# Vision block kernel: the last 64 inner rows of the experts' up layer in plain fp32 on the two row halves

## The reference, cut to what matters

```python
def _L0_ffn_ref(x, router_w, w1, w2):       # x: 2048 tokens x 192
    probs = softmax(xt @ router_w.T)
    topk_w, topk_idx = top_k(probs, 8); topk_w = topk_w / sum(topk_w)
    comb = zeros((T, 16)); comb[t, topk_idx[t]] = topk_w[t]
    for e in range(16):                     # widths: 8 experts of 128, 8 of 256
        h = gelu(xt @ w1[:, off:off + wd])  # up layer, 192 inner rows
        out = out + comb[:, e:e + 1] * (h @ w2[off:off + wd, :])
```

## Time and profile before

| | |
|---|---|
| median of the runs | 721.57 us (721.25 to 721.74) |
| the profiled execution | 722.35 us, of which the span of instructions is 720.5 us |
| TensorE busy | 673.1 us, 93% of the span |
| VectorE busy | 494.9 us, 69% |
| ScalarE busy | 353.7 us, 49% |
| GpSimd busy | 107.3 us, 15% |
| attention part | up to about 477 us |
| expert stage | from there to the end |

### The profile page before, as it was taken

How to read it: one execution, slowest core, us unless ns; L and a number is a source line. 1 busy time by engine, 2 the same in 40 slices (tenths; PEclk the granted TensorE clock), 3 DMA queues, 4 the chain that set the end, 5 groups by cost and what they waited for, 6 DMA issues and landing times.

```text
span 720.5 us, 29763 instructions
## 1 busy us (share of the span) xinstructions
PE 673.1 (93%) x13218; PEld 593.7 (82%) x13218; DVE 494.9 (69%) x1350; ACT 353.7 (49%) x916; POOL 107.3 (15%) x328
## 2 busy tenths in 40 slices
PE   5668999999999999999999999899999999999997
PEld 2557888888888888888888888778999999999996
DVE  5247777777887887778787887667547546646743
ACT  0124565555665665655665656655343443443442
POOL 0121222222222123122123131010000000000000
PEclk9969999999999999999999999999999999999999
DMA  8952111111111111110100000000000000000000
GB/s 310 308 192 61 63 33 32 62 33 34 62 33 34 62 33 35 60 33 32 62 4 4 5 4 5 4 2 1 1 0 23 1 1 23 1 0 23 1 1 22
DMA packets 12255, 30.63 MB, mean 43 GB/s; under 512 B 1120, under 2 KB 7392, under 8 KB 11616
## 3 DMA queue, kind: packets, MB, share of 16 engines
q1 hardware_dynamic: 12128, 28.73, 12.1%
HBM read 27.16 MB, written 1.57 MB: 40 GB/s over the span
## 4 chain that ended last, share of the span: by engine, by line
PE 77%; DVE 15%; ACT 4%; issue 2%; DMA 1%; POOL 0%; DVEq 0%; SPq 0%; POOLq 0%; ACTq 0%
PE ps L371 24%; PE ps L503 17%; PE ps L493 15%; PE ps L270 6%; DVE uu L761 4%; DVE sq L680 3%; PE ps L284 2%; PE ps L321 2%; PE ps L389 2%; PE ps L456 2%; ACT qq L574 2%; DVE rf L768 2%; PE ps L285 1%; ACT rr L578 1%; PE ps L382 1%
## 5 line engine op out<-in xcount | busy, mean ns | idle before, releaser
L820 DVE SCALAR_TENSOR_TENSOR acc<-ps,comb,acc 128x192 f32<-128x192 f32 x256 | 89.1, 410 | 83.9 <-PE ps L503 83.8
L503 PE MATMUL ps<-w_sb,work 128*128 128x192 f32 x768 | 140.4, 326 | 0.7 <-ACT work L651 0.7
L503 PEld LDWEIGHTS ps<-w_sb,work 128*128 128x128 f32 x768 | 129.5, 190 | 9.5 <-issue 1.1
L371 PE MATMUL ps<-rr 64*64 64x64 f32 x3840 | 130.1, 220 | 4.8 <-issue 2.1
L371 PEld LDWEIGHTS ps<-rr 64*64 64x64 f32 x3840 | 118.6, 135 | 17.5 <-ACT rr L578 10.8
L651 ACT ACTIVATE work<-ps 128x512 f32<-128x512 f32 x96 | 57.3, 597 | 137.8 <-PE ps L493 137.8
L574 ACT ACTIVATE qq<-ps 128x384 f32<-128x384 f32 x192 | 92.2, 489 | 63.4 <-PE ps L371 61.2
L761 DVE SCALAR_TENSOR_TENSOR uu<-rr,qq 128x384 f32<-128x384 f32 x160 | 87.8, 558 | 46.2 <-ACT qq L574 40.2
L578 ACT ACTIVATE rr<-ps 128x384 f32<-128x384 f32 x160 | 73.9, 489 | 80.3 <-PE ps L371 79.3
L371 PE MATMUL ps<-uu,qq 64*64 64x64 f32 x4608 | 96.5, 224 | 15.6 <-DVE uu L761 13.7
L371 PEld LDWEIGHTS ps<-uu,qq 64*64 64x64 f32 x4608 | 80.5, 134 | 33.4 <-DVE uu L761 30.2
(11 more groups left out here) (137 smaller groups left out, 1032.5 us busy)
## 6 DMA issues: line engine op xcount, KB each, us to landing
xtb<-xt_dram SPq DMA_DIRECT2D x16, 512.0 KB, 3.6
work<-x_dram SPq DMA_DIRECT2D x16, 512.0 KB, 3.7
wsh<-ws_dram SPq DMA_DIRECT2D x2, 1440.0 KB, 7.7
w_sb<-w_dram SPq DMA_DIRECT2D x1, 2304.0 KB, 25.8
w_a<-w_dram SPq DMA_DIRECT2D x1, 1536.0 KB, 12.5
w_b<-w_dram SPq DMA_DIRECT2D x2, 768.0 KB, 16.7
out_dram<-acc SPq DMA_DIRECT2D x4, 384.0 KB, 2.6
mult<-copies_dram SPq DMA_DIRECT2D x1, 512.0 KB, 13.0
```

The costliest lines, as they stand in the source:

```text
L371: last = pe.matmul(ps[z:z + 64, 2 * lane + i, 64 * j:64 * j + 64], lhs[r, lane, i, j, :], rhs[r, lane, i, j, :], start=True, stop=True)
L503: last = pe.matmul(ps[:, 2 + 2 * (e % 2) + j // 2, (j % 2) * DIM:(j % 2 + 1) * DIM], hid[:, n % 4, j * P:(j + 1) * P], w2_sb[:, c, :], sta ...
L820: last = dve.scalar_tensor_tensor(out=a, in0=ps[:, 2 + 2 * (e % 2) + j // 2, (j % 2) * DIM:(j % 2 + 1) * DIM], scalar=comb[:, g * GT + j, ...
```

## The change

The last 64 inner rows are no longer split into high and low parts. A chunk's full part, `up_full`, keeps the three matmuls on rows 0 to 127. The 64 last rows are one plain fp32 matmul per chunk, `up_half`, straight from w1_b and a new fp32 tile xend; even chunks read the upper half of the partitions (0 to 63), odd chunks the lower half (64 to 127). Two chunks are done together: full, full, half, half. wb is gone, ScalarE and VectorE prepare only wah and wal, ScalarE writes xend beside xhi, and the loops of all three engines step by two chunks, with weights prepared four and five chunks ahead.

```diff
@@ -116,12 +116,12 @@
         acc = sb("acc", [P, NT, DIM])
         comb = sb("comb", [P, NT, EXPERTS])
 
-        xhi, xlo = sb("xhi", [P, 2, NT * P], F32R), sb("xlo", [P, 2, NT * P], F32R)
+        xhi, xlo, xend = sb("xhi", [P, NT * P], F32R), sb("xlo", [P, NT * P], F32R), sb("xend", [P, NT * P])
         hid = work[:].rearrange("p (c n) -> p c n", c=4)
 
         with nc.sbuf_tensor("wsh", [P, 2, 5, 3, DIM], F32) as wsh, nc.sbuf_tensor("whalo", [P, 2, DIM], F32) as whalo:
             pass
-        wah, wal, wb = (sb(n, [P, SLOTS, P], F32R) for n in ("wah", "wal", "wb"))
+        wah, wal = (sb(n, [P, SLOTS, P], F32R) for n in ("wah", "wal"))
 
         ps = ctx.enter_context(nc.psum_tensor("ps", [P, 8, 512], F32))
         A, B, C, D = (ps[:, i, :] for i in (4, 5, 6, 7))
@@ -148,7 +148,7 @@
         q_ready, u_ready, prod_done, r_ready, o_done = sems("q_ready u_ready prod_done r_ready o_done")
         o_copied, proj_done, h2_ready = sems("o_copied proj_done h2_ready")
         tbn_a, tbn_b, trstd, x2_ready, x2tr_done = sems("tbn_a tbn_b trstd x2_ready x2tr_done")
-        x2t_ready, xhi_ready, x2_saved, logits_done = sems("x2t_ready xhi_ready x2_saved logits_done")
+        x2t_ready, xend_ready, xhi_ready, x2_saved, logits_done = sems("x2t_ready xend_ready xhi_ready x2_saved logits_done")
         lmax, lexp, ltop, lrep, lsel, lsum, linv = sems("lmax lexp ltop lrep lsel lsum linv")
         comb_ready, whi_ready, wlo_ready, up_done = sems("comb_ready whi_ready wlo_ready up_done")
         gelu_done, down_done, expert_added = sems("gelu_done down_done expert_added")
@@ -236,7 +236,7 @@
 
             def low_tokens(t):
                 pool.wait_ge(xhi_ready, t + 1)
-                pool.tensor_tensor(xlo[:, :, t * P:(t + 1) * P], x2t[:], xhi[:, :, t * P:(t + 1) * P].bitcast(F32),
+                pool.tensor_tensor(xlo[:, t * P:(t + 1) * P], x2t[:, 0], xhi[:, t * P:(t + 1) * P].bitcast(F32),
                                    ALU.subtract).then_inc(x2_saved, 1)
 
             def iteration(t):
@@ -475,12 +475,12 @@
 
 
             pe.wait_ge(ffw_loaded, 64)
-            def up(n):
+            def up_full(n):
                 g = n // HID
                 if n % HID == 0:
                     pe.wait_ge(x2_saved, (g + 1) * GT)
-                pe.wait_ge(whi_ready, 2 * n + 2)
-                pe.wait_ge(wlo_ready, 2 * n + 2)
+                pe.wait_ge(whi_ready, n + 1)
+                pe.wait_ge(wlo_ready, n + 1)
                 if n >= 3:
                     pe.wait_ge(gelu_done, n - 2)
                 if n == 0:
@@ -488,10 +488,19 @@
                 if n == 1:
                     pe.wait_ge(r_ready, 12 * NT)
                 tok4, k = slice(g * GT * P, (g + 1) * GT * P), n % SLOTS
-                parts = ((wah, xhi, 0), (wah, xlo, 0), (wal, xhi, 0), (wb, xhi, 1), (wb, xlo, 1))
-                for m, (w, xs, half) in enumerate(parts):
-                    last = pe.matmul(ps[:, UPB[n % 3], :], w[:, k, :], xs[:, half, tok4], start=(m == 0), stop=(m == 4))
-                last.then_inc(up_done, 1)
+                for m, (w, xs) in enumerate(((wah, xhi), (wah, xlo), (wal, xhi))):
+                    pe.matmul(ps[:, UPB[n % 3], :], w[:, k, :], xs[:, tok4], start=(m == 0), stop=False)
+
+            def up_half(n):
+                g, r = n // HID, slice(64 * (n % 2), 64 * (n % 2) + 64)
+                tok4 = slice(g * GT * P, (g + 1) * GT * P)
+                pe.matmul(ps[:, UPB[n % 3], :], w1_b[r, n % HID * P:(n % HID + 1) * P], xend[r, tok4], start=False, stop=True).then_inc(up_done, 1)
+
+            def up_pair(n):
+                up_full(n)
+                up_full(n + 1)
+                up_half(n)
+                up_half(n + 1)
 
             def down(n):
                 g, c = divmod(n, HID)
@@ -507,18 +516,19 @@
                 if c == FIRST[e] + WIDTH[e] - 1:
                     last.then_inc(down_done, 1)
 
-            up(0)
+            up_pair(0)
             out_heads(NT - 1)
-            for n in range(NC):
-                if n + 1 < NC:
-                    up(n + 1)
+            for n in range(0, NC, 2):
+                if n + 2 < NC:
+                    up_pair(n + 2)
                 if n == 0:
                     project(NT - 1)
                 if n == 2:
                     transpose_x2(NT - 1)
-                if n == 3:
+                if n == 4:
                     logits(NT - 1)
                 down(n)
+                down(n + 1)
 
 
         @block.scalar
@@ -589,7 +599,8 @@
                     act.wait_ge(x2_saved, t)
                 c = (D if t == NT - 1 else C)[:, 0:2 * P].rearrange("p (a n) -> p a n", a=2)
                 act.activation(x2t[:], c, ACT.Copy).then_inc(x2t_ready, 1)
-                act.activation(xhi[:, :, t * P:(t + 1) * P], c, ACT.Copy).then_inc(xhi_ready, 1)
+                act.activation(xend[:, t * P:(t + 1) * P], c[:, 1], ACT.Copy).then_inc(xend_ready, 1)
+                act.activation(xhi[:, t * P:(t + 1) * P], c[:, 0], ACT.Copy).then_inc(xhi_ready, 1)
 
             def router_exp(t):
                 act.wait_ge(lmax, t + 1)
@@ -597,8 +608,7 @@
 
             def high_part(n):
                 c = n % HID
-                for w, raw in ((wah, w1_a), (wb, w1_b)):
-                    act.activation(w[:, n % SLOTS, :], raw[:, c * P:(c + 1) * P], ACT.Copy).then_inc(whi_ready, 1)
+                act.activation(wah[:, n % SLOTS, :], w1_a[:, c * P:(c + 1) * P], ACT.Copy).then_inc(whi_ready, 1)
 
             def first_window(k, t):
                 if k == 1 and on(t - 1):
@@ -615,10 +625,11 @@
                     exponents(t + 1)
                 if k == 2 and on(t + 1):
                     copy_kernel(t + 1)
-                if k in (0, 1, 2) and t == NT - 1:
-                    if k == 0:
+                if k in (1, 2) and t == NT - 1:
+                    if k == 1:
                         act.wait_ge(ffw_loaded, 64)
-                    high_part(k)
+                    high_part(2 * k - 2)
+                    high_part(2 * k - 1)
                 if k == 3 and on(t - 1):
                     copy_x2(t - 1)
                 if k == 4 and on(t + 2):
@@ -650,16 +661,18 @@
                     act.wait_ge(down_done, g * EXPERTS + EXPERT_OF[c] + 1)
                 act.activation(hid[:, n % 4, :], ps[:, UPB[n % 3], :], ACT.Gelu_apprx_tanh).then_inc(gelu_done, 1)
 
-            for n in range(NC):
+            for n in range(0, NC, 2):
                 gelu(n)
+                gelu(n + 1)
                 if n == 0:
                     copy_out(NT - 1)
-                if n == 3:
+                if n == 4:
                     copy_x2(NT - 1)
-                if n == 5:
+                if n == 6:
                     router_exp(NT - 1)
-                if n + 3 < NC:
-                    high_part(n + 3)
+                for m in (n + 4, n + 5):
+                    if m < NC:
+                        high_part(m)
 
 
         @block.vector
@@ -806,11 +819,10 @@
                 dve.tensor_scalar(comb[:, t, :], rt[:, 3, :], rst[:, 3:4], None, ALU.mult).then_inc(comb_ready, 1)
 
             def low_part(n):
-                dve.wait_ge(whi_ready, 2 * n + 2)
+                dve.wait_ge(whi_ready, n + 1)
                 k, col = n % SLOTS, n % HID * P
-                for w, high, raw, r in ((wal, wah, w1_a, slice(0, P)), (wb, wb, w1_b, slice(DB, P))):
-                    dve.tensor_tensor(w[r, k, :], raw[r, col:col + P], high[r, k, :].bitcast(F32),
-                                      ALU.subtract).then_inc(wlo_ready, 1)
+                dve.tensor_tensor(wal[:, k, :], w1_a[:, col:col + P], wah[:, k, :].bitcast(F32),
+                                  ALU.subtract).then_inc(wlo_ready, 1)
 
             def add_expert(g, e):
                 dve.wait_ge(down_done, g * EXPERTS + e + 1)
@@ -849,9 +861,9 @@
                     router_weights(t - 2)
                 if k == 4 and on(t + 1):
                     start_newton(t + 1)
-                if k in (1, 2, 3) and t == NT - 1:
-                    low_part(k - 1)
-
+                if k in (2, 3) and t == NT - 1:
+                    low_part(2 * k - 4)
+                    low_part(2 * k - 3)
                 if k == 4 and on(t - 1):
                     router_max(t - 1)
                 if k == 5 and on(t + 2):
@@ -907,22 +919,24 @@
             dve.tensor_copy(scrap[:, 2:3], scrap[:, 1:2]).then_inc(expert_added, 1)
             router_weights(NT - 2)
             dve.wait_ge(comb_ready, NT - 1)
-            for n in range(NC):
+            for n in range(0, NC, 2):
                 if n == 0:
                     residual_norm(NT - 1)
-                if n == 1:
+                if n == 2:
                     ffn_input(NT - 1)
-                if n == 5:
+                if n == 6:
                     router_max(NT - 1)
-                if n == 7:
+                if n == 8:
                     router_weights(NT - 1)
                     dve.wait_ge(comb_ready, NT)
```

(14 more changed lines are left out.)

## The result

The changed kernel took 736.46 us (median of five runs, 735.84 to 737.78) against 721.57 us: a ratio of 1.0214, 95% interval 1.0200 to 1.0228. The forecast was 737.5 us. The profiled execution took 737.68 us, its span 735.9 us.

The account below looks back on a forecast made before the run. TensorE's matmul stream was taken to bound the expert stage. A pair grows from 4.91 to 5.25 us, +0.34 times 48 = +16.5 us; with -0.6 us at the edges, 721.6 becomes 737.5 us, range 726 to 759.

Parts of the forecast that it names:

- The bound: Expert stage: it lasts as long as TensorE's stream of matmuls, so savings on neighbouring engines are worth nothing there.
- The arithmetic term: Expert pair on TensorE: two half-rate rounds, 0.87 us, replace four wb matmuls, 0.92 us; -0.055 us a pair.
- Halves beside each other: Expert pair: the two chunks' half matmuls run together on different rows, two rounds (0.87 us) instead of four passes (1.73 us).
- The second rival: Expert pairs: semaphore updates on each matmul keep the halves from meeting; 758 us, or 779 all in a row; chance 0.15.
- The change of shape: Expert pair, into and out of 64-row matmuls: 0.10 us empty plus 0.105 us open weight load each way, 0.40 us.
- The first rival: Expert pairs: TensorE takes 64-row, 128-column matmuls without emptying; a pair costs 4.85 us, total 718.4 us; chance 0.09.
- The light engines at 0: Expert stage: removing 96 ScalarE copies and 96 VectorE subtractions is worth 0, because both engines wait for TensorE.
- The ScalarE copy in the attention part at 0: Attention stage: one more copy (xend) in each of 16 tiles costs 0, with 0.02 us of cover left.
- The third rival: Attention stage: the added ScalarE copy per tile lies on the Newton chain; +1.4 us, 738.9 us, inside the forecast's own range.
- Edges: Expert stage's head and tail: +0.1 us for chunk 1's wait, -0.7 us for a stall gone, tail unchanged; together -0.6 us.
- The stall of 0.67 us: Expert stage's head: TensorE idle at a down group for a GELU late behind a table load; forecast to go, -0.7 us.
- Nothing late next: Expert stage's head: once the late GELU is covered by two down groups, no other wait follows; -0.7 us kept.

Follow-up runs that it names:

- e_light_kept: Changed kernel with ScalarE's 96 copies into wb and VectorE's 96 subtractions put back, though no matmul reads wb: 736.56 us, 1.0210 of the kernel before.
- e_one_half: Changed kernel without the second half matmul of each pair (last 64 inner rows of every odd chunk): 736.48 us, 1.0206 of the kernel before.
- e_rows128: Changed kernel with the last rows' plain fp32 matmuls over all 128 rows, xend's lower half zero: 757.90 us, 1.0500 of the kernel before.
- e_two_visits: Changed kernel with each half matmul cut into two of 256 columns, the second part between the down groups: 756.12 us, 1.0471 of the kernel before.
- e_quads: Changed kernel with four chunks together (full x4, half x4, down x4) from chunk 24 on: 732.79 us, 1.0154 of the kernel before.
- e_order: Changed kernel's paired order, but with the earlier kernel's five fp32r matmuls per chunk and no half matmuls: 721.43 us, 0.9991 of the kernel before.
- e_r_grp: Changed kernel with three fp32r products per chunk on the row halves, all of chunk n issued before n + 1: 729.78 us, 1.0113 of the kernel before.

## Why the prediction was right

- **The bound.** TensorE's stream sets the stage, before and after. Shown: no wait of its down passes, and e_light_kept (0.8 us for 51 us of other engines' work).
- **The arithmetic term**, -0.055 us a pair: two rounds of 0.433 forecast, 0.43 measured, against four matmuls of 0.231, so -0.06. The pass was priced from a row with other columns and all 128 rows, and length scaled with columns alone.
- **Halves beside each other.** Taken from the scores and Newton; shown by the starts, by e_one_half (the second half free) and by e_rows128 (+0.47 us a pair without sharing and without changes). The second rival, halves that do not meet because each carries a semaphore update, did not come: the updates don't hold a neighbour back.
- **The change of shape**, 0.10 + 0.105 us each way, was the term that decided: measured 0.09 and 0.104, doubled by e_two_visits (+19.1 us where 0.205 x 2 x 47 = 19.3), and taken away once in four chunks by e_quads (-0.42 us). The rows it was taken from change to or from 64 rows with 64 columns; that 64 rows with 128 columns cost the same was assumed, and held. The first rival, a free change, is excluded.
- **The light engines at 0.** Right to 0.7 us. Without their saved work the last tile's transpose waits for ffn_input; the prediction had looked at the steady pairs and not at this place.
- **The ScalarE copy in the attention part at 0.** ScalarE's timeline after, the same tile as in the earlier trace rows:

```profile
317.72 0.39 ACT L601 ACTIVATE x2t<-ps 128x256 f32<-128x256 f32 x1
317.98 0.30 ACT L602 ACTIVATE xend<-ps 128x128 f32<-128x128 f32 x1
318.14 0.31 ACT L603 ACTIVATE xhi<-ps 128x128 fp32r<-128x128 f32 x1
318.50 0.49 ACT L584 ACTIVATE qq<-ps 128x384 f32<-128x384 f32 x1
```

x2t, xend and xhi, and the next copy begins 0.78 us after x2t's start, as before. The third rival is excluded: the stage begins at 477.6 us against 477.3.

- **Edges**, -0.6 us forecast. The stage grew by 15.1 us where 48 x (5.24 - 4.91) is 15.8 to 16.0: -0.7 to -0.9. The stall of 0.67 us is gone as forecast, and the full part of chunk 1 begins 0.33 us after the matmul ahead of it instead of 0.23, the +0.1. A part of the rest can be that the first pair's way out of the halves leads to out_heads, where the kernel before changed its shape too (the prediction has its expert stage without any change; that holds behind its head); no run separates that. "Nothing late next" was partly luck: with the work of ScalarE and VectorE kept (e_light_kept) or in the new order alone (e_order) the wait for ffn_input takes the stall's gain away.

The sum came out 1 us high, 737.5 forecast and 736.46 measured: 0.5 us by the pair (16.5 us forecast, 16.0 measured), up to 0.3 by the edges, and the rest is within the scatter of the runs.

## What to carry to other kernels

Row halves fill an idle half of the array, but here each change between 128-row and 64-row matmuls cost about 0.2 us, whatever the columns behind it; count the changes before the savings, and put as much 64-row work as banks allow between two of them. Compare the passes as well: two plain fp32 matmuls on the row halves took 0.86 us a pair, and the four stacked fp32r matmuls that they replaced 0.92, so there was 0.06 us to win and 0.4 us to pay. Work taken off engines that wait for another was worth 0.7 us here, at one place at the stage's head. That place can be worth more than a rearranged inner loop: moving ffn_input shortened the stage by 0.9 us, the best arrangement of halves by 0.3 more.

## What the runs showed of the hardware

- A change of the array's shape between 128 and 64 rows: about 0.09 us with the array empty, and 0.104 us more for the first pass, whose 128 columns of weights are loaded in the open; in both directions (625.35 and 626.41 in the changed kernel) and for fp32r halves too (620.50 in e_r_grp, a first pass of 0.50 against 0.39). Together 0.39 to 0.42 us for in and out (e_rows128, e_two_visits, e_quads).
- Two 64-row matmuls on different row halves, into different banks, take exactly the time of one (group of 1.13 against 1.12 us), and matmuls on one half start ahead of matmuls that were issued before them on the other half, also when they are instructions of their own and one of them updates a semaphore (e_r_grp).
- A pass of 512 columns takes 0.43 us in plain fp32, on 64 rows as on 128, and 0.23 us in fp32r.
